# Self attention of a decoder layer: scores formed twice in eight array tiles, exponentials as weights of the value product

## The chip, the cores and the metric

The kernel runs on one core of one Trainium2 chip. The metric is the device time of one execution in microseconds (us). TensorE (PE in the profile) does the matmuls, VectorE (DVE) and ScalarE (ACT) read and write both memories, GpSimd (POOL) works on SBUF alone, and SyncE (SP) issues most DMA transfers. The engines run their own instruction lists in order and meet at semaphores.

## The reference

One decoder layer with pre-normalisation on x of 16 sequences of 64 tokens of 128 features, float32. Cut to what matters:

```
x = x + self_attn(layernorm(x))      # 16 heads of 8, rotary embedding, biases
x = x + cross_attn(layernorm(x), c)  # 8 heads of 64, context of 64 x 96
x = x + moe(layernorm(x))            # 8 experts, top 2, and 2 shared; 128 -> 176 -> 128

# self_attn
q, k, v = x Wq' + bq, x Wk' + bk, x Wv' + bv
q, k = rope(q) * 8**-0.5, rope(k)
out = softmax(q k') v                # per sequence and head: 64 x 64
return out Wo' + bo
```

## The kernel before

The 1024 tokens are 8 tiles of 128 (two sequences each, `NT` = 8) in two halves. Every engine's list is written out by hand; there is no planner. The stages are: normalisation (`statistics`, `inverse_std`, `normalise`, `transpose_xn`), projections (`queries_keys`, `values`, three half-precision passes each, `mm3`), self attention, its output projection (`project_o`), normalisation again (stages 2, 3 of the arrays `LN`), cross attention in eight units, and the experts in 2 x 14 blocks.

Self attention runs in four quads of four sequences. A quad is four units; a unit u = 4 quad + g has four heads (32 of the 128 features, g) of all four sequences. For a unit, `scores` (L1006) is four matmuls with all 128 features contracted: the queries of the other groups are zeroed (`mask_q`, into `qG`), and the keys of each of the four heads stand in a masked copy (`kM`). The result, 128 x 512, has queries on the partitions. VectorE takes the row maxima (L695) and subtracts them into SBUF (L698), ScalarE takes the exponential (L460), TensorE transposes it (`transpose_p`, L1037), ScalarE copies that into `PT` (`copy_t`, L469), and once per quad `attend` multiplies it by masked values (L1058, 32 matmuls on tiles of 32 columns) and by ones for the row sums (L1064). VectorE divides (`divide_ot`, L712, L716), ScalarE adds the value bias (`bias_ot`). Units follow each other about four deep: three banks for scores, two for transposes, one for the product, and banks 6 and 7 (`MISC`) shared in a fixed order by all other products.

Cross attention uses the same functions with units 16 to 23 (`copy_xq`, `scores`, `shift`, `exponentials`, `sums`, `divide` on POOL, `transpose_p`, `copy_t`, `cross_attend`, `cross_project`). `context_keys` (L950) and `context_values` (L990) are float32 products of the context, spread between units.

The expert weights arrive in 13 chunks through two stage buffers. SP starts the transfer of chunk c when `chunk_lo` is at c - 1, that is when POOL has done `split_chunk` (L332) of chunk c - 2. ScalarE first casts the landed chunk (`chunk_float16`, L425), after which POOL may split it. ScalarE's casts are spread over its list by `CHUNK_AT`, one at most per step of the loop over units. The first expert product waits for all 13.

The hand-over to cross attention is `attend(3)`, `divide_ot(3)`, `bias_ot(3)`, `project_o(1)`, `add_x2(1)`, `statistics(3)`, `inverse_std(3)` on POOL, `normalise(3)`, `transpose_xn(2, 1)`, `cross_queries(1)`.

## Time and profile before

| | |
|---|---|
| median of three runs | 193.68 us (191.53 to 193.82) |
| span of the profiled execution | 190.1 us |
| PE, DVE, ACT, POOL busy | 87%, 71%, 61%, 43% |
| mean granted TensorE clock | 0.986 of full speed |

The span goes from the first to the last instruction of one profiled execution, for which no time of its own is given beside the span; the median stands 3.6 us above it. All start times below are counted from the start of the span. A group of matmuls is best timed from its start to the start of the next group, since the ends are modelled. A float32 matmul leaves two records, each with its own weight load. When TensorE is busy throughout a stretch, what the other engines do there costs nothing by itself.

### The profile page before, as it was taken

The page shows a single profiled execution, that of the slowest core. Times are in us where ns is not written, and L with a number is a line of the kernel's source. Part 1 is how long each engine was busy: PE and PEld are TensorE (multiplying, and loading weights), DVE is VectorE, ACT ScalarE, POOL GpSimd, SP SyncE. Part 2 cuts the span into 40 slices and gives each one's busy share as a digit, 9 for nine tenths or more (in the row PEclk, how much of TensorE's full clock was granted, in tenths as well). Part 3 has the DMA queues.
Part 4 walks back from the last instruction along what each step waited for, and adds up shares of the span by engine and source line. Part 5 has one row for each costly group of instructions (what it writes and reads, how often), then busy time and mean ns, then how long its engine had stood idle before and what let it go on. Part 6 is the DMA issues. An engine that isn't in the chain of part 4 may idle for free.

```text
span 190.1 us, 4163 instructions
## 1 busy us (share of the span) xinstructions
PE 165.1 (87%) x1599; PEld 103.2 (54%) x1599; DVE 134.7 (71%) x279; ACT 115.7 (61%) x227; POOL 81.8 (43%) x78
## 2 busy tenths in 40 slices
PE   7576985999999689849999799997998799999992
PEld 2134543665657346635757687653664566666661
DVE  3468998969989627986184554888787987556642
ACT  2148178795788385658779974653649344555450
POOL 1459560847445000763052440074443455544540
PEclk9999999999999999996999999999999999999997
DMA  5980000031221200100000000000000001000001
GB/s 143 304 280 0 0 2 3 0 84 56 59 58 57 78 0 3 59 14 2 10 0 3 2 3 0 0 5 0 0 3 2 0 3 38 17 0 3 2 3 55
DMA packets 6900, 6.43 MB, mean 34 GB/s; under 512 B 736, under 2 KB 5312, under 8 KB 6880
## 3 DMA queue, kind: packets, MB, share of 16 engines
q1 hardware_dynamic: 6480, 5.63, 10.0%
q10 hardware_dynamic: 400, 0.53, 0.9%
q8 instruction: 13, 0.21, 0.5%
q14 instruction: 7, 0.06, 0.1%
HBM read 5.63 MB, written 0.52 MB: 32 GB/s over the span
## 4 chain that ended last, share of the span: by engine, by line
PE 53%; DVE 16%; ACT 14%; issue 7%; POOL 5%; DMA 3%; POOLq 1%; DVEq 0%; ACTq 0%
PE bank L930 6%; PE bank L1006 6%; PE bank L932 6%; PE bank L931 6%; DVE xn_sb L638 4%; PE bank L1175 4%; PE bank L1037 4%; PE bank L1100 4%; ACT Vx L487 3%; PE bank L1110 3%; DMA x_sb<-x_dram 3%; PE bank L1179 2%; POOL rstd L310 2%; PE bank L1159 2%; ACT ex L460 2%
## 5 line engine op out<-in xcount | busy, mean ns | idle before, releaser
L339 POOL TENSOR_TENSOR qG<-qG 128x512 f16<-128x512 f32 (+1 forms) x26 | 30.1, 1157 | 38.4 <-ACT qG L527 38.3
L520 ACT ACTIVATE qG<-bank 128x512 f32<-128x512 f32 (+1 forms) x28 | 16.7, 597 | 24.4 <-PE bank L932 24.4
L798 DVE TENSOR_TENSOR qG<-bank,qG 128x512 f32<-128x512 f32 (+1 forms) x28 | 19.3, 690 | 13.0 <-PE bank L932 11.5
L695 DVE TENSOR_REDUCE mx<-bank 128x8 f32<-128x512 f32 x24 | 16.3, 680 | 6.1 <-PE bank L1022 4.5
L527 ACT CAST qG<-qG 128x512 f16<-128x512 f32 (+1 forms) x28 | 17.1, 612 | 5.5 <-DVE qG L802 3.5
L460 ACT ACTIVATE ex<-sh 128x512 f32<-128x512 f32 x24 | 15.2, 632 | 6.6 <-DVE sh L698 6.5
L1006 PE MATMUL bank<-kM,qG 128*64 128x256 f32 x128 | 16.9, 390 | 1.3 <-DVE qG L679 1.3
L1175 PEld LDWEIGHTS bank<-wd_sb,qG 128*128 128x128 f16 (+1 forms) x224 | 14.7, 98 | 6.2 <-ACT qG L527 0.7
L698 DVE TENSOR_TENSOR sh<-bank,mx 128x512 f32<-128x512 f32 x24 | 16.6, 692 | 1.6 <-ACT ex L460 0.8
L1175 PE MATMUL bank<-wd_sb,qG 128*128 128x128 f16 (+1 forms) x224 | 17.1, 219 | 0.6 <-ACT qG L527 0.6
L802 DVE TENSOR_TENSOR qG<-bank,qG 128x512 f32<-128x512 f32 x22 | 15.2, 692 | 0.7
L1037 PE MATMUL bank<-consts_sb,ex 128*128 128x128 f32 x96 | 14.8, 277 | 0.0
L1037 PEld LDWEIGHTS bank<-consts_sb,ex 128*128 128x128 f32 x96 | 11.1, 141 | 6.3 <-issue 5.3
L332 POOL TENSOR_TENSOR wd_sb<-stage,wd_sb 128x512 f16<-128x512 f32 (+2 forms) x5 | 4.3, 864 | 20.7 <-ACT wd_sb L425 20.7
L487 ACT COPY Vx<-bank 64x256 f32<-64x256 f32 x32 | 11.7, 367 | 2.3 <-PE bank L990 1.9
L346 POOL TENSOR_TENSOR ex<-ex,rs 128x512 f32<-128x512 f32 x8 | 8.4, 1044 | 11.0 <-DVE rs L707 11.0
L469 ACT COPY PT<-bank 128x512 f32<-128x512 f32 x16 | 9.3, 586 | 3.9 <-PE bank L1037 3.8
L950 PE MATMUL bank<-ctxT_sb,xwk_sb 128*128 128x512 f32 x16 | 10.4, 738 | 1.3 <-issue 1.3
L1006 PEld LDWEIGHTS bank<-kM,qG 128*64 128x64 f32 x128 | 8.0, 136 | 6.4 <-issue 2.2
L1100 PE MATMUL bank<-PTx,Vx 128*64 128x128 f32 x128 | 9.6, 296 | 2.0 <-ACT PTx L478 2.0
L414 ACT ACTIVATE kxM<-bank,consts_sb 128x512 f32<-128x512 f32 x16 | 10.0, 684 | 1.7 <-PE bank L950 1.7
L1179 PE MATMUL bank<-wd_sb,qG 128*128 128x128 f16 (+1 forms) x112 | 10.8, 219 | 0.1
(131 smaller groups left out, 380.7 us busy)
## 6 DMA issues: line engine op xcount, KB each, us to landing
stage<-w_gate_dram SPq DMA_DIRECT2D x3, 256.0 KB, 6.6
stage<-w_up_dram SPq DMA_DIRECT2D x3, 256.0 KB, 2.6
stage<-w_down_dram SPq DMA_DIRECT2D x3, 256.0 KB, 2.9
x_sb<-x_dram SPq DMA_DIRECT2D x2, 256.0 KB, 5.7
out_dram<-x_sb SPq DMA_DIRECT2D x2, 256.0 KB, 2.3
ctxT_sb<-ctxT_dram ACTq DMA_DIRECT2D x1, 384.0 KB, 4.7
sel_sb<-selector_dram SPq DMA_DIRECT2D x1, 352.0 KB, 6.4
qG<-attn_w_dram SPq DMA_DIRECT2D x1, 320.0 KB, 5.9
```

What stands on the lines that cost most here:

```text
L339: nc.gpsimd.tensor_tensor(hs[0:r, u % 2, 1, :], hh[0:r, u % 2, :], hs[0:r, u % 2, 0, :], ALU.subtract).then_inc(h_lo, 1)
L460: nc.scalar.activation(ex[:, u % NE, :], sh[:, u % 2, :], ACT.Exp, scale=SCALE1 if u < NU1 else SCALE2).then_inc(e_ready, 1)
L487: ins = nc.scalar.copy(Vx[h2 * S:(h2 + 1) * S, 2 * p + b2, :, :], src)
L520: nc.scalar.activation(sg[0:r, u % 2, :], gbank(u)[0:r, :], ACT.Silu).then_inc(sg_ready, 1)
L527: nc.scalar.copy(hs[0:r, u % 2, 0, :], hh[0:r, u % 2, :]).then_inc(h_hi, 1)
L695: link(nc.vector.reduce_max(mx[:, u % 2, :], v, AX.X))
L698: nc.vector.tensor_tensor(sh[:, u % 2, :].rearrange("p (c t) -> p c t", t=S), v, mx[:, u % 2, :].unsqueeze(2).broadcast_to([P, BLK, S]), A ...
L798: nc.vector.tensor_tensor(dst, ubank(u)[0:r, :], sg[0:r, u % 2, :], ALU.mult).then_inc(hu_ready, 1)
L1006: ins = mm(sbank(u)[b2 * S:(b2 + 1) * S, pp * HG * S:(pp + 1) * HG * S], qG[:, g, b * S:(b + 1) * S], kM[:, b].rearrange("p i t -> p (i t) ...
L1037: ins = nc.tensor.transpose(tbank(u)[:, c * P:(c + 1) * P], ex[:, u % NE, c * P:(c + 1) * P], ident)
L1100: ins = mm(o[c * S:(c + 1) * S, j, :, b2, :], Vx[:, 2 * p + b2, hp, :], PTx[:, u % 2, 2 * hp + b2, :, :], start=True, stop=True)
L1175: mm(pvb[:, n * P:(n + 1) * P], hs[0:r, u % 2, 0, n * P:(n + 1) * P], w[s], start=(first and n == 0 and s == 0), stop=False, skip_group_ch ...
```

## The change

Scores are formed twice. `first_scores` makes them as before in layout, queries on the partitions, but contracts only the 32 features of the group, on array tiles of 32 rows and 64 columns, each group with a bank of its own (0 to 3), so that q needs no mask. `maxima` (VectorE) takes the row maxima of a unit and writes them, 8 per row, into columns of `ms`. After four units `transpose_max` turns these to rows (eight transposes), ScalarE copies them (`copy_mT`), and `shifted_scores` forms the scores again with the keys on the partitions: first minus the maximum (one row contracted, eight matmuls of 512 columns), then k q (sixteen matmuls of 256 columns, q now masked by head) accumulated onto it, in the same banks. ScalarE takes the exponential straight from those banks into `PT`, so the subtraction, the transposes of the exponentials and their copies are gone. `attend` has the exponentials as weights (64 columns) and 18 moving columns: 8 values and a one for each of two sequences, which gives the row sums. `divide_o` divides, `turn_o` transposes back (two transposes), `bias_ot` copies with the bias. `project_o` contracts 64 rows at a time, on the diagonal tiles, with w_o in a new layout.

Around it: the mask of the queries goes from VectorE (first quad) to POOL, all quads; `PTx` now lies in `PT` and is zeroed after the third quad; the raw projection weights are staged in `PT`; a third shared bank (5) joins `MISC`; and every engine's list is written anew. In particular the casts of the weight chunks stand elsewhere in ScalarE's list and the splits elsewhere in POOL's.

```diff
-        VM = sb("VM", [P, 2, NT, G, 2, 32])
+        V1 = sb("V1", [P, NT, H1, 2, D1 + 1])
-        sbank = lambda u: bank[u % 3]
-        tbank = lambda u: bank[3 + u % 2]
+        qbank = lambda g: bank[g]
+        sbank = lambda p: bank[p % 3]
+        tbank = lambda p: bank[3 + p % 2]
+        ob = bank[4]
...
@@ POOL
+            mask_q(0)
+            mask_k(1)
+            mask_q(1)
...
+            mask_k(2)
             mask_q(2)
-            mask_k(2)
+            mask_k(3)
+            mask_q(3)
             for c in range(3):
                 split_chunk(c)
-            mask_q(3)
-            mask_k(3)
-            for c in range(3, 8):
+            pool.wait_ge(pv_full, 3)
+            nc.gpsimd.memset(PT[:, 0:4, :], 0.0).then_inc(zeroed, 1)
+            inverse_std(2)
+            x2_bias(0)
+            for c in range(3, 9):
                 split_chunk(c)
-            inverse_std(2)
-            split_chunk(8)
-            x2_bias(0)
-            for u in range(NU1, NU):
-                divide(u)
-                if u == 16:
+            for p in range(NT):
+                divide(p)
+                if p == 0:
                     inverse_std(3)
-                if u == 17:
+                if p == 1:
                     split_chunk(9)
                     split_chunk(10)
...
@@ ACT
+            def copy_mT(quad):
+                for pp in range(2):
+                    act.wait_ge(mT_full, 2 * quad + pp + 1)
+                    nc.scalar.copy(mT[:, pp].rearrange("p i b s -> p (i b s)"), qbank(pp)[:, :]).then_inc(mT_copied, 1)
...
+            for quad in range(4):
+                copy_mT(quad)
+                if quad == 0:
                     copy_v(0)
...
+                if quad == 3:
+                    copy_cv(2)
+                for g in range(G):
+                    exponentials(4 * quad + g)
...
+                if quad == 1:
+                    bias_ot(0)
+                    copy_v(1)
+                    chunk_float16(0)
+                if quad == 2:
+                    bias_ot(1)
+                    copy_kx(3)
+                    chunk_float16(1)
+                    chunk_float16(2)
+                if quad == 3:
                     bias_ot(2)
+                    copy_cv(3)
+                    chunk_float16(3)
+            copy_kx(4)
+            copy_xnT(2, 0)
+            bias_ot(3)
+            copy_xq(0)
+            copy_kx(5)
+            copy_kx(6)
+            for c in range(4, 8):
+                chunk_float16(c)
+            cross_exponentials(0)
+            chunk_float16(8)
+            cross_exponentials(1)
+            chunk_float16(9)
+            copy_kx(7)
+            copy_t(0)
+            copy_xnT(2, 1)
+            copy_cv(4)
+            cross_exponentials(2)
+            chunk_float16(10)
...
@@ DVE
+            def maxima(u):
+                quad, g = u // 4, u % 4
...
+                dve.wait_ge(first_full, u + 1)
+                nc.vector.reduce_max(ms[:, :, 32 * g], qbank(g)[:, :].rearrange("p (c t) -> p c t", t=S),
+                                     AX.X).then_inc(max_ready, 1)
...
+                if quad == 3:
+                    divide_o(2)
                     add_x2(0)
                     statistics(2, x2_sb)
+                    divide_o(3)
                     normalise(2, x2_sb)
                     rest_xnT(2)
+            shift(0)
+            shift(1)
+            sums(0)
+            add_x2(1)
+            statistics(3, x2_sb)
+            sums(1)
+            normalise(3, x2_sb)
...
@@ PE
+            def first_scores(quad):
...
+                for g in range(G):
+                    if quad:
+                        pe.wait_ge(e_ready, 4 * (quad - 1) + g + 1)
+                    r = slice(32 * g, 32 * (g + 1))
+                    for pp in range(2):
+                        for b2 in range(2):
+                            b = 4 * quad + 2 * pp + b2
+                            t = (2 * pp + b2) * S
+                            ins = mm(qbank(g)[b2 * S:(b2 + 1) * S, pp * HG * S:(pp + 1) * HG * S],
+                                     qr[r, quad % 2, t:t + S], kM[r, b].rearrange("p i t -> p (i t)"),
+                                     start=True, stop=True)
+                    ins.then_inc(first_full, 1)
+
+            def transpose_max(quad):
+                pe.wait_ge(max_ready, 4 * quad + 4)
+                for pp in range(2):
+                    for i in range(HG):
+                        ins = nc.tensor.transpose(qbank(pp)[:, i * P:(i + 1) * P], ms[:, pp * HG + i, :], ident)
+                    ins.then_inc(mT_full, 1)
+
+            def shifted_scores(quad):
+                pe.wait_ge(mT_copied, 2 * quad + 2)
+                pe.wait_ge(q_masked, quad + 1)
+                for b2 in range(2):
+                    for g in range(G):
+                        mm(qbank(g)[b2 * S:(b2 + 1) * S, :], minus_one[32 * g:32 * g + 1, :],
+                           mT[32 * g:32 * g + 1].rearrange("p a i b s -> p (a i) b s")[:, :, b2, :],
+                           start=True, stop=False, skip_group_check=True)
+                for pp in range(2):
+                    for b2 in range(2):
+                        for g in range(G):
+                            r = slice(32 * g, 32 * (g + 1))
+                            t = (2 * pp + b2) * S
+                            ins = mm(qbank(g)[b2 * S:(b2 + 1) * S, pp * HG * S:(pp + 1) * HG * S],
+                                     kr[r, quad % 2, t:t + S], qG[r, :, quad * QT + t:quad * QT + t + S],
+                                     start=False, stop=bool(pp), skip_group_check=True)
+                            if pp and b2:
+                                ins.then_inc(shifted_full, 1)
...
             def attend(quad):
-                pe.wait_ge(t_copied, 4 * quad + 4)
+                pe.wait_ge(e_ready, 4 * quad + 4)
...
+                    pe.wait_ge(ot_ready, quad)
...
+                    for h in range(H1):
+                        ptg = PT[:, (4 * quad + h // HG) % NPT, :].rearrange("p (q i s) -> p q i s", q=2, i=HG)
+                        at = (pp * (H1 // 2) + h // 2) * 2 * (D1 + 1)
+                        ins = mm(ob[h % 2 * S:(h % 2 + 1) * S, at:at + 2 * (D1 + 1)], ptg[:, pp, h % HG, :],
+                                 V1[:, 2 * quad + pp, h].rearrange("p b d -> p (b d)"), start=True, stop=True)
...
+            first_scores(1)
+            attend(0)
+            transpose_max(1)
             context_keys(2)
+            shifted_scores(1)
+            turn_o(0)
+            values(1)
+            queries_keys(3)
+            first_scores(2)
+            attend(1)
+            transpose_max(2)
+            context_values(1)
+            shifted_scores(2)
+            turn_o(1)
             context_keys(3)
+            context_values(2)
+            first_scores(3)
+            attend(2)
+            transpose_max(3)
+            project_o(0)
+            shifted_scores(3)
+            turn_o(2)
+            context_values(3)
+            context_keys(4)
+            attend(3)
+            turn_o(3)
+            transpose_xn(2, 0)
+            cross_queries(0)
+            context_keys(5)
+            cross_scores(0)
+            cross_scores(1)
+            context_keys(6)
+            project_o(1)
+            cross_scores(2)
+            cross_scores(3)
+            context_keys(7)
             transpose_p(0)
+            context_values(4)
+            transpose_xn(2, 1)
+            transpose_p(1)
+            cross_attend(0)
+            cross_queries(1)
...
```

## Rows read from the trace of the kernel before

**Rows 1.** The page, busy us, share of the span and instructions of each engine.
```profile
PE 165.1 (87%) x1599; PEld 103.2 (54%) x1599; DVE 134.7 (71%) x279; ACT 115.7 (61%) x227; POOL 81.8 (43%) x78
```
**Rows 2.** Windows of self attention: stretch, length, busy us (instructions) per engine, clock, DMA.
```profile
core 0: us, PE busy (x) PEld busy (x) DVE busy (x) ACT busy (x) POOL busy (x), PEclk, DMA share, GB/s
32.40:62.00 29.60, 29.60 (x421) 18.26 (x420) 26.19 (x48) 23.23 (x52) 16.75 (x14) 1.00 0.19 53
```
**Rows 3.** Timeline of the start: start us, us, engine, line, operation, idle before.
```profile
16.09 1.71 ACT L452 ACTIVATE kM<-qkr,consts_sb 128x256 f32<-128x256 f32 x4 [0.63 <-DVE qkr L672]
...
19.07 2.81 PE L1006 MATMUL bank<-kM,qG 128*64 128x256 f32 x24 [1.34 <-DVE qG L679]
...
19.72 1.10 DVE L638 TENSOR_SCALAR xn_sb<-x_sb,mv,rstd 128x128 f32<-128x128 f32 x4
```
**Rows 4.** Timeline of TensorE, one unit and one attend.
```profile
43.34 1.10 PE L1058 MATMUL bank<-PT,VM 128*32 128x64 f32 x64
44.26 1.05 PE L1064 MATMUL bank<-PT,consts_sb 128*32 128x256 f32 x16
45.24 0.66 PE L1037 MATMUL bank<-consts_sb,ex 128*128 128x128 f32 x4
45.83 1.08 PE L1006 MATMUL bank<-kM,qG 128*64 128x256 f32 x8
46.84 1.13 PE L990 MATMUL bank<-xwv_sb,ctxT_sb 128*128 128x512 f32 x2
```
**Rows 5.** Timeline of TensorE, groups that follow each other on the full array.
```profile
64.30 1.02 PE L950 MATMUL bank<-ctxT_sb,xwk_sb 128*128 128x512 f32 x2
65.16 0.60 PE L1037 MATMUL bank<-consts_sb,ex 128*128 128x128 f32 x4
65.60 0.38 PE L930 MATMUL bank<-xnT,xwq_sb 128*128 128x512 f16 x1
```
**Rows 6.** Groups by line: count, busy us, mean ns of one, idle before.
```profile
L695 DVE TENSOR_REDUCE mx<-bank 128x8 f32<-128x512 f32 x24 | 16.3, 680 | 6.1 <-PE bank L1022 4.5 <-PE bank L1006 1.4
L698 DVE TENSOR_TENSOR sh<-bank,mx 128x512 f32<-128x512 f32 x24 | 16.6, 692 | 1.6 <-ACT ex L460 0.8
L712 DVE RECIPROCAL rsum<-bank 128x256 f32<-128x256 f32 x4 | 7.0, 1753 | 0.5 <-PE bank L1064 0.4
L469 ACT COPY PT<-bank 128x512 f32<-128x512 f32 x16 | 9.3, 586 | 3.9 <-PE bank L1037 3.8
```
**Rows 7.** A chunk's cast and split (timeline), then transfers: KB, us to landing.
```profile
39.28 0.62 ACT L425 CAST wg_sb<-stage 128x512 f16<-128x512 f32 x1
39.97 1.16 POOL L332 TENSOR_TENSOR wg_sb<-stage,wg_sb 128x512 f16<-128x512 f32 x1 [1.08 <-ACT wg_sb L425]
...
stage<-w_up_dram SPq DMA_DIRECT2D x3, 256.0 KB, 2.6
stage<-w_down_dram SPq DMA_DIRECT2D x3, 256.0 KB, 2.9
```
**Rows 8.** Timeline of the hand-over to cross attention, by engine.
```profile
76.82 1.13 PE L1076 MATMUL bank<-wo_sb,t 128*128 128x128 f32 x8 [0.89 <-ACT t L494]
...
78.64 1.05 POOL L346 TENSOR_TENSOR ex<-ex,rs 128x512 f32<-128x512 f32 x1
80.39 0.23 POOL L308 TENSOR_SCALAR ve<-mv 128x4 f32<-128x4 f32 x1 [0.70 <-DVE mv L627]
80.70 1.04 POOL L310 TENSOR_TENSOR rstd<-ve,minus_half 128x4 f32<-128x4 f32 x1
...
81.78 2.68 DVE L638 TENSOR_SCALAR xn_sb<-x_sb,mv,rstd 128x128 f32<-128x128 f32 x4 [0.52 <-POOL rstd L310]
...
84.61 0.63 PE L959 MATMUL bank<-consts_sb,xn_sb 128*128 128x128 f32 x4 [2.40 <-DVE xn_sb L638]
```
**Rows 9.** Sixteen passes twice (timeline), and the clock in 40 slices (page).
```profile
85.60 1.97 PE L1100 MATMUL bank<-PTx,Vx 128*64 128x128 f32 x16
93.82 1.07 PE L1100 MATMUL bank<-PTx,Vx 128*64 128x128 f32 x16
...
PEclk9999999999999999996999999999999999999997
```

More of the change, by code:

```diff
@@ L182, in decoder_layer @@
         pool_c = sem("pool_c")
[L183 to L184 removed]
+        misc_full = [sem(f"misc_full{i}") for i in range(3)]
+        misc_free = [sem(f"misc_free{i}") for i in range(3)]
         gw_split = sem("gw_split")
@@ new lines, in copy_t @@
+            def copy_t(p):
+                act.wait_ge(t_full, p + 1)
+                if p == 0:
+                    act.wait_ge(zeroed, 5)
+                if p >= 2:
+                    act.wait_ge(pv_full, 4 + p - 2 + 1)
+                src = tbank(p)[:, :].rearrange("p (c s) -> p c s", s=S)
+                for j in range(2):
+                    r = slice(j * S, (j + 1) * S)
+                    ins = nc.scalar.copy(PTx[r, p % 2, :, j, :], src[r])
+                ins.then_inc(t_copied, 1)
@@ new lines, in _ @@
+            copy_xq(1)
+            copy_t(1)
+            copy_otx(0)
+            cross_exponentials(3)
+            copy_cv(5)
+            for p in range(4, NT + 3):
+                if p < NT:
+                    cross_exponentials(p)
+                if p - 2 < NT:
+                    copy_t(p - 2)
+                copy_otx(p - 3)
+                if p in (4, 5):
+                    copy_cv(p + 2)
+                    chunk_float16(p + 7)
+                if p == NT + 1:
+                    copy_xnT(3, 0)
@@ L829, in _ @@
             rotate(0)
-            mask_q0()
             normalise(1, x_sb)
-            for j in range(NU + 4):
-                if j < NU:
-                    shift(j)
-                if 0 <= j - 5 - NU1 < NT:
-                    add_x3(j - 5 - NU1)
-                if NU1 < j < NU and j not in (18, 20):
-                    sums(j - 1)
-                if j == NU - 1:
-                    sums(j)
-                if j == 17:
-                    add_x2(1)
-                    statistics(3, x2_sb)
-                    sums(17)
-                    normalise(3, x2_sb)
-                if j == 0:
+            for quad in range(4):
+                for g in range(G):
+                    maxima(4 * quad + g)
+                if quad == 0:
+                    rest_xnT(1)
                     rotate(1)
-                    rest_xnT(1)
-                if j == 2:
-                    mask_k1()
-                if j == 3:
+                if quad == 1:
                     rotate(2)
-                if j == 8:
-                    rotate(3)
-                if j == 10:
+                    divide_o(0)
                     dve.wait_ge(ld["gw"], 16)
@@ L1074, in project_o @@
                 for n in range(TPH):
-                    t = (hf * TPH + n) * P
-                    ins = mm(ps[:, n * P:(n + 1) * P], OT[:, t:t + P], wo_sb[:, :], start=True, stop=True)
+                    for i2 in range(2):
+                        for b2 in range(2):
+                            r = slice(b2 * S, (b2 + 1) * S)
+                            ins = mm(ps[r, n * P:(n + 1) * P], OT[r, hf * TPH + n, i2, :], wo_sb[r, i2, :],
+                                     start=(i2 == 0), stop=(i2 == 1), skip_group_check=True)
                 ins.then_inc(full, 1)
@@ new lines, in _ @@
+            first_scores(0)
+            transpose_xn(1, 1)
+            queries_keys(1)
+            transpose_max(0)
+            values(0)
+            shifted_scores(0)
+            queries_keys(2)
+            context_values(0)
+            first_scores(1)
+            attend(0)
+            transpose_max(1)
+            context_keys(2)
+            shifted_scores(1)
[4 more added lines that the diff above has]
+            attend(1)
@@ L1256, in _ @@
+            context_values(5)
+            cross_scores(6)
+            cross_project(0)
+            context_values(6)
+            transpose_p(3)
+            cross_attend(2)
+            cross_scores(7)
+            cross_project(1)
+            context_values(7)
+            for p in range(4, NT):
+                transpose_p(p)
+                cross_attend(p - 1)
+                cross_project(p - 2)
             transpose_xn(3, 0)
```

545 lines of the change are left out of this document (212 added, 333 removed).

## The prediction

> **What bounds the kernel now.** I read the busy shares first, then the slices and stretches, then the order of time on each engine where self attention hands over to cross attention. TensorE is busy for 87% of the span [rows 1], and from 32.4 to 62 us, where most of self attention runs, for all 29.60 us of the stretch [rows 2]. So in that stage an edit on VectorE or ScalarE is worth nothing by itself; it must shorten TensorE's list. At two places the stage is set by a chain across engines instead: the start (rotation, mask, first scores) [rows 3], and the hand-over at 76.8 to 84.6 us: `project_o(1)`, the residual, `normalise(3)`, `transpose_xn(2, 1)` [rows 8]. After `transpose_xn(2, 1)` both kernels have the same work in nearly the same order, up to the end. I therefore predict the moment at which that transpose starts (84.61 us now) and carry the difference to the end.
>
> **TensorE, per quad of four units.** Removed: four units of scores at 1.01 us (45.83 to 46.84), four groups of transposes at 0.59 (45.24 to 45.83; where the same tile shape follows they take 0.44 [rows 5]), so about 0.52 on average, and one `attend` at 0.92 + 0.98 (43.34, 44.26, 45.24) [rows 4]. Sum 4.04 + 2.1 + 1.9 = 8.0 us.
> The pieces of the new list come from passes. A float32 matmul is two passes (two records); 512 columns take 0.43 us per pass, since two take 0.86 [rows 5], so 256 columns take 0.213. The four matmuls of a unit are 8 such passes, 1.7 us if they ran in turn; they take 1.01, so the two column halves overlap, with 0.16 for the change of tile shape. The 64 passes of `attend`'s first part (64 columns, 0.053 us each) take 0.92 us, so four column tiles overlap fully [rows 4].
> - `first_scores`: sixteen matmuls of 32x64 tiles. In the written order each row group holds two rounds, and the next group's first round can only join the second one of the group before: five rounds of 2 x 0.213, 2.13 + 0.16 = 2.3 us. If row groups do not overlap it stays at 4 x 1.01 = 4.0; below 1.8 (four rounds) the order excludes.
> - `transpose_max`: 8 transposes at 0.11 [rows 5] = 0.9.
> - `shifted_scores`: eight K = 1 matmuls of 512 columns, all on different tiles, 0.86; then two rounds of eight, 0.86; with the change 1.9. No row shows two row groups at once. The upper end is no overlap: here the row group is the inner loop, so even the column halves no longer pair: 8 x 0.86 + 16 x 0.43 = 13.7. I take 1.9: the nearest rows are the column tiles, which overlap two and four at a time without loss [rows 4], and each row group has a bank of its own.
> - new `attend`: 32 matmuls, 64 passes, 64-column weights, only 18 moving columns. Weight loads are the limit. Lower end: a pass as cheap as now, 0.92 us. Upper end: the present passes load 32 columns each, on four tiles, in 0.92; if only different tiles load at once, twice the columns on half the tiles is four times, 3.7. I take 2.2, near the middle of the two because the present rows are bound by streaming and leave the load between these ends.
> - `turn_o`: 2 x 0.11 + 0.16 = 0.4.
> Sum 7.7 us against 8.0: a saving of 0.3 per quad, 1.2 in all. `project_o` goes from 8 passes on the full array to 32 on 64x64 tiles, two at a time: 16 x 0.107 + 0.16 = 1.85 us instead of 1.13 [rows 8], +1.4 for both. **TensorE's list is as long as before.**
>
> The Trainium skill, TensorE: Matmul & The Clock Gate (Part 3, packing), says that matmuls in different row groups run at once, a four-row packing at 3.07 times; by it `shifted_scores` is 1.9 to 2.5. No row here shows that for rows of the array. The Trainium skill, TensorEngine Tiling (Instruction Overhead), speaks against the 18 moving columns: each matmul costs some 60 cycles whatever its width, which by an estimate is 64 x 25 ns = 1.6 us for the new `attend`; the 64 passes in 0.92 us are already below that floor, so the trace does not bear it out across column tiles [rows 4].
>
> **VectorE and ScalarE.** VectorE loses 16 subtractions (0.69) and four reciprocals of 256 elements (1.75) for ones of 32 elements: 11 + 6 us less [rows 6]. ScalarE loses 16 copies and gains 8 (0.59 each), 4.7 us less [rows 6]. Cover: TensorE's full list hides both, so I count nothing. Masking for q moves from VectorE to POOL: scores start when the key mask ends (16.09 + 1.71 = 17.8) instead of 19.07 [rows 3], -1.2 us; but the projections that filled TensorE there come later.
>
> **The schedule that follows.** A quad's period is 7.7 us plus the projections between (12 half-precision passes of 256 columns at half the float32 price, 1.3, and two float32 matmuls of 512, 1.7) = 10.7. Quad 0 is a bare chain: first scores at 17.8, `normalise(1)` 1.1 to 2.1 and four maxima up to 22, transposes and two copies up to 24.1, shifted scores up to 26, then 2.2 us of projections. So the first scores of quad 1, 2, 3 begin at about 28, 39 and 50; maxima (4 x 0.68), copies and exponentials fit under the other work. Quad 3 has no later quad beside it: exponentials and `bias_ot(2)` hold `attend(3)` until 62, it ends at 64; `normalise(2)` now stands behind `divide_o(3)` on VectorE, so `cross_queries(0)` starts near 68 (65.60 now [rows 5]). `project_o(1)` ends at about 77, against 77.9. The lead from the start is gone by here.
>
> **The step that decides: the weight chunks on ScalarE.** Two stage buffers serve 13 chunks. A chunk can be cast when it has landed; its transfer starts when POOL has split the chunk two before. Now the casts are spread over the kernel. In the new order ScalarE casts chunks 4, 5, 6, 7 in a row after `copy_kx(6)`, then `cross_exponentials(0)`, chunk 8, `cross_exponentials(1)`. `copy_kx(6)` ends at about 76 (its matmul stands ahead of `project_o(1)`). From there, with 0.07 for each handing-over, as 39.90 to 39.97 [rows 7]:
> cast 4 0.69, split 4 1.23, transfer 6 2.67, cast 6 0.67, split 6 1.23, transfer 8 2.97, cast 8 0.67, split 8 1.16 = 11.3 us. Then on POOL `divide(0)` 1.04 and `inverse_std(3)` 1.35, and on VectorE `normalise(3)` 1.1 to 2.7 (2.68 now, beside POOL [rows 8]; the same four instructions took 1.10 with POOL idle [rows 3]). Sum 14.8 to 16.4; 15.5 taken.
> So `transpose_xn(2, 1)` starts at 76 + 15.5 = 91.5 instead of 84.61: **+6.9 us**. Who is queued behind: `cross_exponentials(0)` (shift ready at 74 to 75) waits for casts 6 and 7 until about 82; `sums(0)` and behind it on VectorE `add_x2(1)` and `statistics(3)`; on POOL `divide(0)` and `inverse_std(3)` behind split 8; on TensorE `transpose_p(0)`. SP's queue holds only these transfers.
> TensorE then idles for about 8 us. Now its clock goes to the lower of its two levels, 1.2 GHz, after an idle 2.4 us ending at 84.61 [rows 8]; 16 passes take 1.97 instead of 1.07, and the slice shows a granted 0.6 [rows 9]. It will drop again, earlier; some 10 passes more at half speed: 0 to 2 us, 0.5 taken.
> **Sum:** +7.4 us on the 190.1 span, 197.5. The median of the runs stands 3.6 above the span, which I keep: about 201.0 us.
>
> **Rivals.**
> (a) The chunk wait bites but TensorE's new pieces are at their low ends (`attend` 0.92, first scores 1.8): the period falls by 1.5 before maxima and copies become the bound, `copy_kx(6)` ends near 71.5, transpose at 86.3 to 88: +1.7 to +3.5, 195.4 to 197.2. For it: full overlap of column tiles now. Chance 0.18.
> (b) **Faster**: as (a), and casts 4 to 7 find their chunks ready. They cost 4 x 0.6 = 2.4 us, and the chain from `project_o(1)` (end 73) to the transpose takes the 6.7 us of now: 79.9, -4.7, 189.0. It needs transfer 6 landed when ScalarE comes to it, which the wait of SP on split 4 excludes unless ScalarE is late by some 4 us elsewhere. It decides once the chain from cast 4 is under 8 us. Chance 0.06.
> (c) Weight loads bind: `attend` at 3.7, first scores at 3.0 (between 2.3 and 4.0): +2.2 per quad, three periods and the tail, +8: 209. For it: float32 loads are never seen without a stream over them. Chance 0.15.
> (d) The eight tiles do not run at once: first scores 4.0, shifted 13.7: +13.5 per quad, 54 in all, 255. Against it: column tiles do overlap. Chance 0.05.
>
> **Numbers.** My forecast has 0.56: 201.0 us, itself 197.5 to 205. The range takes in (a) from 195.4 less a little for the schedule, and (c): 194.5 to 209. A change under 2% (3.9 us) cannot be told from none: that is up to 197.6, which holds (a) and a small part of the forecast. Faster 0.06, same 0.20, slower 0.74.
>
> **What would show it.** Right: in the new profile ScalarE idle before the casts of chunks 6 and 8 with a transfer as releaser, 2 to 3 us each; VectorE's `ls` reduction waiting for ScalarE near 80; TensorE idle for 6 us or more ahead of `transpose_xn(2, 1)`, with the granted clock below 1 there. Shifted scores from 1.8 to 2.5 us per quad; the stage from first to last self attention full of TensorE. Wrong: no idle at those casts (b); a shifted group of over 4 us (d); `attend` over 3 us (c). I am also wrong if the work after the transpose has slack that takes up the delay.

## The result, and the profile after

| | before | after |
|---|---|---|
| median of the runs on one chip | 192.9 us (191.53 to 193.82) | 201.95 us (201.16 to 203.9) |
| ratio, 95% interval | | 1.0494 [1.0411, 1.0576] |
| span of the profiled execution | 190.1 us | 202.1 us |
| mean granted TensorE clock | 0.986 | 0.910 |

The change makes the kernel slower by some 5%. The profiled execution of after took 203.9 us and is the longest of its four; the other three have spans of 199.4 to 200.8 us and clocks of 0.932 to 0.949. So start times read from its trace make the delay look 1 to 3 us larger than it typically is.

The page of after, busy shares and the 40 slices:

```profile
PE 166.7 (82%) x1751; PEld 108.1 (53%) x1751; DVE 119.8 (59%) x259; ACT 110.8 (55%) x211; POOL 85.2 (42%) x83
...
PE   7284998989896599406999879998899789999992
...
PEclk9858599999999679965599999999999999999997
```

Against [rows 1], VectorE has lost 15 us of work and ScalarE 5, and the time went the other way. TensorE's busy time rose by only 1.6 us, part of that being passes at the low clock. The two digits to look at are the 4 and the 0 of TensorE, about 81 to 91 us: it stands still for most of that time. Its clock has three low places where [rows 9] has one.

TensorE's timeline in self attention, two first scores and what lies between (half-precision projections left out):

```profile
30.73 1.16 PE L1031 MATMUL bank<-kM,qkr 32*64 32x256 f32 x32
31.82 2.05 PE L1113 MATMUL bank<-V,PT 128*64 128x18 f32 x64
...
34.47 1.09 PE L1041 MATMUL bank<-consts_sb,sh 128*128 128x128 f32 x8 [0.60 <-DVE sh L717]
...
36.35 1.11 PE L1050 MATMUL bank<-ex,consts_sb 1*64 1x512 f32 x16
37.26 1.07 PE L1058 MATMUL bank<-qG,qkr 32*64 32x256 f32 x32
...
38.75 0.44 PE L1121 MATMUL bank<-consts_sb,On 128*128 128x128 f32 x2 [0.42 <-DVE On L746]
...
41.10 1.16 PE L1031 MATMUL bank<-kM,qkr 32*64 32x256 f32 x32
```

`first_scores` takes 31.82 - 30.73 = 1.09 us, `attend` 2.05 and the shifted scores 0.91 + 1.00 = 1.91. From one quad's first scores to the next are 10.4 us here and 10.1 from quad 2 to quad 3 (51.21). TensorE now waits 0.60 us for the maxima in each of the quads 1 to 3 and 0.42 us for `divide_o` in two of them, where it never waited in [rows 2].

The hand-over, TensorE:

```profile
62.62 2.05 PE L1113 MATMUL bank<-V,PT 128*64 128x18 f32 x64 [0.69 <-ACT OT L520]
...
69.36 0.58 PE L957 MATMUL bank<-xnT,xwq_sb 128*128 128x512 f16 x1 [1.52 <-issue]
...
78.04 1.96 PE L1134 MATMUL bank<-wo_sb,OT 64*64 64x128 f32 x32
...
91.63 1.12 PE L1094 MATMUL bank<-consts_sb,ex 128*128 128x128 f32 x4 [8.67 <-POOL ex L358]
...
95.76 1.09 PE L984 MATMUL bank<-consts_sb,xn_sb 128*128 128x128 f32 x4 [1.30 <-DVE xn_sb L671]
```

`project_o(1)` ends near 80, 2 to 3 us later than the forecast (77) and than before (77.9); `transpose_xn(2, 1)` starts at 95.76 against 84.61 in [rows 8]. In between TensorE waits 8.67 us for POOL. The same hand-over on ScalarE, from `copy_kx(6)` on:

```profile
78.15 1.27 ACT L435 ACTIVATE kxM<-bank,consts_sb 128x512 f32<-128x512 f32 x2 [1.69 <-PE bank L975]
79.30 1.14 ACT L446 CAST wu_sb<-stage 128x512 f16<-128x512 f32 x2
83.76 0.62 ACT L446 CAST wu_sb<-stage 128x512 f16<-128x512 f32 x1 [3.32 <-DMA stage<-w_up_dram]
84.65 0.38 ACT L446 CAST wu_sb<-stage 128x224 f16<-128x224 f32 x1 [0.28 <-DMA stage<-w_up_dram]
84.94 0.62 ACT L492 ACTIVATE ex<-sh 128x512 f32<-128x512 f32 x1
88.72 0.62 ACT L446 CAST wd_sb<-stage 128x512 f16<-128x512 f32 x1 [3.16 <-DMA stage<-w_down_dram]
```

and on VectorE and POOL:

```profile
85.59 0.69 DVE L735 TENSOR_REDUCE ls<-ex 128x8 f32<-128x512 f32 x1 [6.63 <-ACT ex L492]
...
92.93 2.68 DVE L671 TENSOR_SCALAR xn_sb<-x_sb,mv,rstd 128x128 f32<-128x128 f32 x4 [2.03 <-POOL rstd L320]
...
89.42 1.16 POOL L344 TENSOR_TENSOR wd_sb<-stage,wd_sb 128x512 f16<-128x512 f32 x1 [3.24 <-ACT wd_sb L446]
...
91.86 1.04 POOL L320 TENSOR_TENSOR rstd<-ve,minus_half 128x4 f32<-128x4 f32 x1
```

Read it from the DMA side: ScalarE waits for chunks 6, 7 and 8 (3.32, 0.28, 3.16 us), its exponentials come late, VectorE's `sums(0)` waits for them, and POOL's `divide(0)` and `inverse_std(3)` stand behind the split of chunk 8. The whole chain from the first of the four casts (79.30) to the transpose is 16.46 us.

Behind the transpose no slack takes up the delay. The first expert product starts here in before and in after:

```profile
119.86 0.38 PE L930 MATMUL bank<-xnT,wg_sb 128*128 128x512 f16 x1
...
131.85 0.38 PE L957 MATMUL bank<-xnT,wg_sb 128*128 128x512 f16 x1
```

The transpose is 11.15 us late, the first expert product 11.99 and the end of the span 12.0.

Windows of after, with the granted clock as the last column but two; rows come in order of time:

```profile
core 0: us, PE busy (x) PEld busy (x) DVE busy (x) ACT busy (x) POOL busy (x), PEclk, DMA share, GB/s
...
18.27:26.54 8.27, 7.44 (x68) 5.91 (x69) 8.20 (x14) 1.76 (x3) 3.36 (x2) 0.59 0.01 2
26.54:62.60 36.06, 32.73 (x594) 21.76 (x593) 20.18 (x45) 23.95 (x52) 20.24 (x15) 1.00 0.07 20
...
66.80:73.60 6.80, 5.27 (x15) 2.07 (x16) 0.69 (x1) 2.50 (x6) 0.00 (x0) 0.51 0.03 11
```

The lower level, 1.2 GHz, holds in parts of the first quad (granted 0.59 on the mean of the row), for 6.8 us that take in `cross_queries(0)` (behind 62.6 to 66.8 us, in which TensorE was busy for 2.48 of 4.20 us), and after the long wait.

### The profile page after: what moved, and what is told of

Read it like the earlier page. It is cut to its first block, busy times and chain, and to the rows that moved or that the text cites. A ratio compares the mean times of both kernels' runs of the same rounds, so it can differ in the third digit from the quotient of the medians.

```text
span 202.1 us, 4385 instructions
## 1 busy us (share of the span) xinstructions
PE 166.7 (82%) x1751; PEld 108.1 (53%) x1751; DVE 119.8 (59%) x259; ACT 110.8 (55%) x211; POOL 85.2 (42%) x83
## 4 chain that ended last, share of the span: by engine, by line
PE 51%; DVE 17%; issue 10%; ACT 10%; POOL 6%; DMA 4%; POOLq 1%; DVEq 0%; ACTq 0%
PE bank L957 7%; PE bank L958 7%; PE bank L959 7%; DVE xn_sb L671 5%; PE bank L1236 4%; PE bank L1161 3%; DVE sh L717 3%; PE bank L1171 3%; DVE t L693 2%; DMA x_sb<-x_dram 2%; PE bank L984 2%; PE bank L975 2%; PE bank L1240 2%; PE bank L1220 2%; PE bank L1080 2%
## 5 line engine op out<-in xcount | busy, mean ns | idle before, releaser
L830 DVE TENSOR_TENSOR qG<-bank,qG 128x512 f32<-128x512 f32 (+1 forms) x28 | 19.3, 690 | 12.9 <-PE bank L959 11.5
L717 DVE TENSOR_REDUCE sh<-bank 128x8 f32<-128x512 f32 x16 | 9.9, 684 | 10.6 <-PE bank L1031 10.6
L735 DVE TENSOR_REDUCE ls<-ex 128x8 f32<-128x512 f32 x8 | 5.5, 682 | 14.9 <-ACT ex L492 14.9
L1094 PE MATMUL bank<-consts_sb,ex 128*128 128x128 f32 x32 | 5.8, 311 | 8.7 <-POOL ex L358 8.7
L335 POOL TENSOR_TENSOR kM<-qkr,consts_sb 128x1024 f32<-128x1024 f32 x3 | 5.7, 1894 | 14.9 <-DVE qkr L707 14.9
L435 ACT ACTIVATE kxM<-bank,consts_sb 128x512 f32<-128x512 f32 x16 | 10.1, 692 | 2.3 <-PE bank L975 2.2
L344 POOL TENSOR_TENSOR wu_sb<-stage,wu_sb 128x512 f16<-128x512 f32 (+1 forms) x4 | 4.0, 1020 | 17.3 <-ACT wu_sb L446 17.3
L1161 PE MATMUL bank<-PT,Vx 128*64 128x128 f32 x128 | 9.6, 296 | 2.0 <-ACT PT L504 2.0
L671 DVE TENSOR_SCALAR xn_sb<-x_sb,mv,rstd 128x128 f32<-128x128 f32 x16 | 8.6, 600 | 3.7 <-POOL rstd L320 3.7
L504 ACT COPY PT<-bank 64x512 f32<-64x512 f32 x16 | 9.3, 580 | 2.7 <-PE bank L1094 2.6
L1220 PE MATMUL bank<-wT,sel_sb 128*128 128x512 f16 x22 | 8.4, 381 | 2.9 <-DVE qG L834 2.9
L984 PE MATMUL bank<-consts_sb,xn_sb 128*128 128x128 f32 x24 | 5.5, 374 | 6.2 <-DVE xn_sb L671 6.2
```

The lines of the kernel that those rows point to most:

```text
L671: ins = nc.vector.tensor_scalar(xn_sb[:, hf, n, :], src[:, hf * TPH + n, :], mv[:, hf, n, 0:1], rstd[:, hf, n:n + 1], ALU.subtract, ALU.mult)
L717: nc.vector.reduce_max(ms[:, :, 32 * g], qbank(g)[:, :].rearrange("p (c t) -> p c t", t=S), AX.X).then_inc(max_ready, 1)
L830: nc.vector.tensor_tensor(dst, ubank(u)[0:r, :], sg[0:r, u % 2, :], ALU.mult).then_inc(hu_ready, 1)
L1161: ins = mm(o[c * S:(c + 1) * S, j, :, b2, :], Vx[:, 2 * p + b2, hp, :], PTx[:, p % 2, 2 * hp + b2, :, :], start=True, stop=True)
```

## The experiments

The theory (A): the bunched casts on two stage buffers hold the exponentials, the sums and POOL, and through them `transpose_xn(2, 1)`. Rivals: (B) TensorE's new list is itself longer or slower; (C) the place of `project_o(1)` and `normalise(2)` in the lists costs it, with the chunks late beside it.

**Five stage buffers**, nothing else moved:

```
-        stage = [sb(f"stage{i}", [P, CH]) for i in range(2)]
+        stage = [sb(f"stage{i}", [P, CH]) for i in range(5)]
...
-                if c >= 2:
-                    sp.wait_ge(chunk_lo, c - 1)
+                if c >= 5:
+                    sp.wait_ge(chunk_lo, c - 4)
```

> The changed kernel with five stage buffers for the weight chunks instead of two; no engine's order is touched. Theory A (ScalarE stands on transfers of chunks 6 and 8, which start only after the splits two before): the idle time of 3.3, 0.3 and 3.2 us before those casts goes, the hand-over is then set by POOL's five splits in a row, transpose_xn(2, 1) starts near 90.3 instead of 95.8, and the time falls by 5 to 6 us, to about 196.5. Rival B (the low TensorE clock and the new tiles set the hand-over, the transfers only stand beside it): less than 1.5 us. Rival C (the delay has slack later in cross attention): the transpose is earlier, the end is not.

Measured: 197.35 us (196.09 to 197.89), ratio to before 1.0237 [1.0140, 1.0333]. ScalarE, POOL and TensorE in it:

```profile
77.76 1.93 ACT L446 CAST wu_sb<-stage 128x512 f16<-128x512 f32 x4
79.59 0.63 ACT L492 ACTIVATE ex<-sh 128x512 f32<-128x512 f32 x1
...
78.45 3.96 POOL L344 TENSOR_TENSOR wu_sb<-stage,wu_sb 128x512 f16<-128x512 f32 x4 [15.29 <-ACT wu_sb L446]
...
88.71 0.63 PE L984 MATMUL bank<-consts_sb,xn_sb 128*128 128x128 f32 x4 [2.61 <-DVE xn_sb L671]
```

The four casts run without a wait, and the transpose is 7.0 us earlier than in after. Of these, 1.5 us lie ahead of the casts (they start at 77.76 instead of 79.30), where this edit does nothing; the chain from the first cast to the transpose is 10.95 us instead of 16.46. 4.6 us of the time are back, and by the ratios to before (1.0494 and 1.0237) that is half of the loss. The bunching isn't gone with the buffers: POOL still has five splits in a row ahead of `divide(0)`, from 78.45 to 83.5. So the waits for transfers make up about half of the loss; this kernel does not say what makes up the rest.

**The casts spread again** (two buffers; casts 4 to 7 one by one between the copies of `kx` and `xq`, 8 and 9 further back, split 8 behind `divide(1)`):

```
             copy_kx(4)
+            chunk_float16(4)
             copy_xnT(2, 0)
             bias_ot(3)
+            chunk_float16(5)
             copy_xq(0)
+            chunk_float16(6)
             copy_kx(5)
+            chunk_float16(7)
             copy_kx(6)
-            for c in range(4, 8):
-                chunk_float16(c)
...
```

> The changed kernel with two stage buffers, but ScalarE's casts of chunks 4 to 9 spread over copy_kx(4) to copy_t(0), and POOL's split of chunk 8 moved behind divide(1). Theory A: no cast waits long, POOL is free for divide(0) and inverse_std(3); transpose_xn(2, 1) starts near 87.6 and the time falls by about 8 us, to 194, within 1% of the kernel before. Rival B: less than 1.5 us. If only the order on POOL counts and not the transfers, this gains and five buffers do not.

Measured: 195.91 us (194.18 to 197.13), ratio 1.0193 [1.0082, 1.0303]. VectorE and TensorE, `add_x2(1)` first:

```profile
80.47 0.65 DVE L759 TENSOR_TENSOR x_sb<-bank,xb_sb 128x512 f32<-128x512 f32 x1
...
83.92 3.54 DVE L674 TENSOR_SCALAR xn_sb<-x_sb,mv,rstd 128x128 f32<-128x128 f32 x4 [0.51 <-POOL rstd L320]
...
87.60 0.63 PE L987 MATMUL bank<-consts_sb,xn_sb 128*128 128x128 f32 x4 [3.68 <-DVE xn_sb L674]
```

and `add_x2(1)` in before:

```profile
78.33 0.65 DVE L724 TENSOR_TENSOR x_sb<-bank,xb_sb 128x512 f32<-128x512 f32 x1
```

6.0 us are back from the order of the casts and of one split alone (0.61 of the loss by the ratios). The time is 1.9 us above what was expected. Three us of the delay against before are left at the transpose. Of these, `add_x2(1)` is 2.14 us late: `project_o(1)` ends at 79.60 instead of 77.88, and `sums(0)` stands ahead of it. The other 0.86 us are `normalise(3)`, 3.54 us beside POOL instead of 2.68. The first part fits (C); this kernel does not test (C) by itself.

**The same fault put into the kernel before** (casts 4 to 7 bunched, splits 3 to 8 behind each other, `mask_q(3)`, `mask_k(3)`, `inverse_std(2)` and `x2_bias(0)` ahead of them on POOL):

```
+                    for c in range(4, 8):
+                        chunk_float16(c)
...
-        CHUNK_AT = [3, 4, 7, 8, 10, 11, 12, 13, 16, 17, 18, 20, 21]
+        CHUNK_AT = {7: (0,), 11: (1, 2), 15: (3,), 16: (8,), 17: (9,), 18: (10,), 20: (11,), 21: (12,)}
```

> The kernel before, with its weight chunks cast and split in the places of the changed kernel (chunks 4 to 7 in a row before the first cross exponential, 8 and 9 behind the next two, splits 3 to 8 ahead of divide). Theory A: chain from cast 4 at 71.2 us gives transpose_xn(2, 1) at 86 to 88 instead of 84.6, and bias_ot(2) is late too: 3 to 5 us slower, 196 to 198. Rival: the bunching costs only together with the new attention; then no change (under 1 us).

Measured: 200.29 us (198.99 to 201.22), ratio 1.0394 [1.0285, 1.0502]. ScalarE and TensorE:

```profile
78.75 0.62 ACT L423 CAST wu_sb<-stage 128x512 f16<-128x512 f32 x1 [2.96 <-DMA stage<-w_up_dram]
79.71 0.62 ACT L423 CAST wu_sb<-stage 128x512 f16<-128x512 f32 x1 [0.34 <-DMA stage<-w_up_dram]
82.63 0.38 ACT L423 CAST wu_sb<-stage 128x224 f16<-128x224 f32 x1 [2.31 <-DMA stage<-w_up_dram]
...
86.15 2.05 PE L1076 MATMUL bank<-wo_sb,t 128*128 128x128 f32 x8 [6.45 <-ACT t L492]
...
94.62 0.63 PE L959 MATMUL bank<-consts_sb,xn_sb 128*128 128x128 f32 x4 [1.43 <-DVE xn_sb L638]
```

Waits of the same kind appear in a kernel that has none of the new matmuls, here before the casts of chunks 5, 6 and 7. They cost 3.9%, and the time is over the 196 to 198 expected: `bias_ot(3)` and with it `project_o(1)` also stand behind the casts, which they do not in after. So the bunching costs without the new matmuls too. It doesn't measure what (B) adds in after; the kernel with the mended order below does.

**The head filled**: `queries_keys(1)` ahead of `first_scores(0)`, so that TensorE has work while the maxima are taken.

```
             queries_keys(0)
-            first_scores(0)
-            transpose_xn(1, 1)
             queries_keys(1)
+            first_scores(0)
+            transpose_xn(1, 1)
...
```

> The changed kernel with queries_keys(1) ahead of first_scores(0), in the 2.3 us for which TensorE stood idle before them. If the head is set by the low clock (transposes of the maxima at 1.7 us instead of 0.9, projections at 2.6 instead of 1.3), the shifted scores of quad 0 start 1 to 2 us earlier and the time falls by as much. Rival: the head is set by VectorE's chain (normalise, maxima); then under 0.5 us.

Measured: 200.25 us (199.82 to 201.59), ratio 1.0408 [1.0312, 1.0505], against 1.0494 for after: 1.7 us back. The start of quad 1 moves from 30.73 to:

```profile
28.43 1.16 PE L1031 MATMUL bank<-kM,qkr 32*64 32x256 f32 x32
```

Not all of that need be the edit. The kernels with five buffers and with spread casts have the old head, and quad 1 starts at 28.99 and 30.04 in their traces; the low clock fell differently in each. The intervals of the two ratios overlap.

**Both edits**, the spread casts and the filled head:

> The changed kernel with the spread casts and splits, and queries_keys(1) ahead of first_scores(0). The two edits act at different places (the hand-over and the head), so they add up: 195.9 less 1.7 = 194.2 us, no different from the kernel before within 1%. If both only moved the phase of the clock, the sum is not reached and the time stays at 195.5 or above.

Measured: 197.16 us (195.05 to 198.06), ratio 1.0249 [1.0161, 1.0337]. The gains do not add: this is no better than the spread alone, and the two intervals overlap. Windows of this kernel:

```profile
10.00:20.00 10.00, 7.08 (x62) 4.18 (x62) 7.88 (x24) 5.14 (x10) 7.47 (x8) 1.00 0.32 118
...
86.60:92.40 5.80, 5.80 (x29) 3.85 (x30) 3.99 (x7) 3.61 (x8) 1.44 (x2) 0.50 0.16 45
```

and the same stretches of the kernel with the spread casts alone:

```profile
10.00:20.00 10.00, 6.32 (x50) 3.59 (x50) 7.74 (x23) 5.13 (x10) 7.38 (x9) 0.67 0.33 120
...
86.60:92.40 5.80, 3.87 (x32) 2.44 (x33) 4.98 (x9) 4.05 (x9) 1.43 (x2) 1.00 0.19 57
```

The low clock has left the start and has come in at 86.6 to 92.4 us, where TensorE is busy throughout. The full clock would have done those 5.8 us of work in about half. The lead of the filled head is smaller: 1.65 us at the start of quad 1 (28.39 against 30.04), 1.0 us at the transpose (86.60 against 87.60). In both kernels TensorE has just waited 3.68 us at the transpose, and only in one of them the clock falls. These are single executions, and the mean clock of this kernel goes from 0.934 to 0.960 from one to the next. That one low spell took the place of the other is seen in these two; why, and how often, is not settled.

**One row group**: all scores use rows 0 to 31 of the array, so row groups cannot overlap. It leaves out that each group needs its own features and maxima. It was timed once.

```
-                    r = slice(32 * g, 32 * (g + 1))
+                    r = slice(0, 32)
...
```

> The changed kernel with all scores on row group 0 (features 0 to 31 for all four groups, so the attention weights are not the reference's); as many matmuls of the same sizes, on two array tiles instead of eight. If the row groups overlap fully in the change, first scores go from 1.1 to 3.6 us a quad and shifted scores from 1.9 to 7.0, +7.6 a quad, +25 to +30 us in all. If the row groups never overlapped (and column halves did), nothing changes.

Measured: 266.85 us, span 265.0, clock 0.828. TensorE's timeline, the first scores of the second quad (`attend` follows at 48.52):

```profile
44.92 3.67 PE L1031 MATMUL bank<-kM,qkr 32*64 32x256 f32 x32
```

and its windows over the shifted scores of the first quad:

```profile
28.78:33.69 4.91, 4.91 (x23) 2.32 (x25) 1.03 (x1) 1.24 (x2) 4.55 (x4) 1.00 0.00 0
33.69:41.60 7.91, 7.91 (x30) 4.07 (x27) 0.00 (x0) 1.57 (x3) 1.29 (x1) 0.50 0.00 0
```

First scores take 3.60 us instead of 1.09. The shifted ones take 4.91 us at the full clock and 7.91 at half of it, 8.9 at the full clock (4.91 + 7.91 / 2) instead of 1.91. So the change does have its eight tiles at work together. The group was expected to take 7.0 and the kernel 25 to 30 us more; it took 64.9 more. That the group takes 8.9 is between two column halves that always pair (7.0) and none that do (the prediction's 13.7), which would be so if some pair; no row shows which. By an estimate the row groups give 4 x (2.5 + 7.0) = 38 us. The clock gives some 27: a mean of 0.828 over 265.0 us holds back 45.6 us, 0.910 over 202.1 us 18.2. It fell to 0.50 at 33.69 us, after 4.91 us in which TensorE was busy throughout, on two of its eight tiles at most.

**Twice the moving columns in `attend`**, 36 instead of 18 (the extra ones are another head's values and make the product a different one). It was timed once.

```
-                        ins = mm(ob[h % 2 * S:(h % 2 + 1) * S, at:at + 2 * (D1 + 1)], ptg[:, pp, h % HG, :],
-                                 V1[:, 2 * quad + pp, h].rearrange("p b d -> p (b d)"), start=True, stop=True)
+                        ins = mm(ob[h % 2 * S:(h % 2 + 1) * S, at:at + 4 * (D1 + 1)], ptg[:, pp, h % HG, :],
+                                 V1[:, 2 * quad + pp, min(h, 14):min(h, 14) + 2].rearrange("p h b d -> p (h b d)"), start=True, stop=True)
```

> The changed kernel with 36 moving columns instead of 18 in each matmul of attend (each overwrites half of its neighbour's, so the output is not the reference's). If attend's 32 ns per pass is the load of 64 float32 weight columns, its 2.05 us stay. If moving columns or their fixed cost set it, it rises: two tiles with 36 columns at two cycles each need 15 ns per pass, so a rise would have to come from there, to 3 us or more.

Measured: 201.03 us, span 199.2, and

```profile
30.13 2.06 PE L1113 MATMUL bank<-V,PT 128*64 128x36 f32 x64
```

18 more moving columns cost nothing. What is left are the 64 weight loads of 64 columns or a fixed cost of each pass; the two are not told apart. Either way a pass takes 32 ns, the change of tile shape included, or 64 ns on each of the two column tiles.

**The order mended**: head filled, `normalise(2)` and `transpose_xn(2, 0)` ahead of `divide_o(3)` and `turn_o(3)`, `project_o(1)` right behind `cross_queries(0)`, `add_x2(1)`, `statistics(3)` and `normalise(3)` ahead of the sums, `inverse_std(3)` on POOL ahead of the divisions, and the casts one at a time. `transpose_xn(2, 1)` itself stands earlier in TensorE's list, ahead of `context_keys(7)`, `cross_scores(3)`, `context_values(4)` and `transpose_p(0)`. The matmuls are those of the change.

```
+            transpose_xn(2, 0)
             turn_o(3)
-            transpose_xn(2, 0)
             cross_queries(0)
+            project_o(1)
             context_keys(5)
             cross_scores(0)
             cross_scores(1)
             context_keys(6)
-            project_o(1)
             cross_scores(2)
+            transpose_xn(2, 1)
+            context_keys(7)
             cross_scores(3)
-            context_keys(7)
+            context_values(4)
             transpose_p(0)
-            context_values(4)
-            transpose_xn(2, 1)
...
+                    normalise(2, x2_sb)
                     divide_o(3)
-                    normalise(2, x2_sb)
                     rest_xnT(2)
+            add_x2(1)
+            statistics(3, x2_sb)
             shift(0)
+            normalise(3, x2_sb)
...
             copy_xq(0)
             copy_kx(5)
+            chunk_float16(5)
+            cross_exponentials(0)
             copy_kx(6)
-            for c in range(4, 8):
-                chunk_float16(c)
...
```

> The changed kernel's instructions in a new order: head filled as above, turn_o behind its cover, normalise(2) and transpose_xn(2, 0) ahead of divide_o(3) and turn_o(3), project_o(1) right after cross_queries(0) (shared bank 5), with add_x2(1), statistics(3) and normalise(3) before any sum, and one cast at most between two exponentials. If the hand-over was only queued work on the wrong side of waits, transpose_xn(2, 1) starts at 76 to 80 us instead of 95.8 and the time is 184 to 190, faster than the kernel before. Rival: ScalarE's list (copies of q, keys, exponentials) is then the bound of this part, little is gained over the spread order: 192 or more.

Measured: **188.36 us** (186.3 to 191.33), ratio to before 0.9715 [0.9595, 0.9835]: faster than both kernels, though the interval does not rule out a gain of under 2%. TensorE:

```profile
68.77 1.96 PE L1140 MATMUL bank<-wo_sb,OT 64*64 64x128 f32 x32
...
76.44 0.63 PE L990 MATMUL bank<-consts_sb,xn_sb 128*128 128x128 f32 x4 [0.67 <-DVE xn_sb L677]
```

and its window of the hand-over:

```profile
62.00:76.00 14.00, 12.53 (x159) 8.01 (x156) 7.10 (x22) 9.79 (x20) 4.17 (x5) 1.00 0.15 40
```

The transpose starts 19.3 us earlier than in after and 8.2 earlier than in before, and the clock holds at 1.00 through the whole hand-over. The time falls by 13.6 us against after and by about 5.5 against before. So rival (B) is answered: the new matmuls do not by themselves make the kernel slower. Of the lead of 8.2 us in the two profiled executions 3.2 are left at the first expert product (116.63 against 119.86) and at the end. The 5 us between are products that stood ahead of the transpose in before and now stand behind it (3.4 us) and longer waits, mostly for ScalarE's copies (5.6 us against 2.8), less the 1.7 us that the low clock held back in before (granted 0.81 over 84.61 to 93.82 us).

**The mended order with five stage buffers:**

> The reordered kernel with five stage buffers. Theory: in the reordered kernel (188.36 us) ScalarE never waits for a chunk any more (its waits from 60 to 95 us are all for products or shifts), so three more buffers are worth nothing: 187.9 to 188.9 us, transpose_xn(2, 1) at 76.0 to 76.9. Rival: a late chunk still holds something that the rows do not name, or the later transfers disturb others: 185 to 187, or over 190.

Measured: 188.19 us (186.43 to 190.1), ratio 0.9710 [0.9618, 0.9802]. As the theory had it, the buffers are worth nothing once no cast waits. The transpose, at 77.87 us, misses its expected 76.9; the profiled execution is the longest of its four (190.1 us).

**The mended order with the old head:**

> The reordered kernel with the changed kernel's head (first_scores(0) ahead of queries_keys(1)). Theory: since the head's gain was lost in the spread version (197.16 against 195.91), the hand-over order is what made the reordered kernel fast, and the head is worth its 1.7 us at most: 188.4 to 190.1 us. Rival: with the waits further on gone, the list of TensorE binds from the head to the end, and the whole 2.3 us by which quad 1 starts later comes back, with more behind it through the clock: 190.7 to 192.5.

Measured: 188.81 us (188.71 to 189.52), ratio 0.9780 [0.9716, 0.9845]; the transpose is at 77.28. The head is worth 0.45 us by the medians and 1.3 us by the ratios to before, the fairer measure here, since before itself stood at 193.8 us beside this kernel and at 193.0 beside the other. Both lie within the intervals. Nearly all of what made the kernel fast is the rest of the new order.

## Why the prediction was right, and where its terms were off

- **The step that decides** was right in place and in kind. Waits of 2 to 3 us at the casts of chunks 6 and 8 were forecast, and are 3.32 and 3.16; `sums(0)` waits as named; TensorE's 8 us are 8.67. The chain of 15.5 us measured 16.46, just over its upper end of 16.4, with `normalise(3)` at its dear price of 2.68. Five buffers and the spread casts show that the bunching is the cause of half to two thirds of the loss (4.6 and 6.0 of 9.0 us); the fault in the old kernel shows that it costs there too. The rest of the loss is put down to the order around it (C), since the mended order brings it all back; that kernel moved many things at once.
- **`copy_kx(6)`** was to end at 76 and ends at 79.42. This is the term that was mis-sized. The prediction had the low clock once, behind the long wait, for 0.5 us. It comes three times: in the first quad (first scores of quad 1 at 30.73 instead of 28, of which it is a part), in `cross_queries(0)`, where 5.27 us of matmuls run at 0.51, and behind the wait. The first two stand ahead of the casts. Of the 2.7 us at the start of quad 1 only 0.6 are left at `attend(3)` (62.62 instead of 62), because the quads were shorter than forecast; `cross_queries(0)` starts 1.4 late (69.36 instead of 68) and takes 4.72 us, where its 12 passes of 512 columns at half the float32 price are 2.6. Together that is the delay of 3.4 us.
- **`first_scores`** was set at 2.3 us, with 1.8 as the least the written order allows. It takes 1.09: 32 passes of 0.213 us on eight tiles are four rounds of one pass each, 0.85, and some 0.2. The trace has the 32 starts of quad 1 in four groups of eight, at 30.73 to 30.81, 30.99 to 31.08, 31.21 to 31.30 and 31.43 to 31.51 us. So a matmul whose tile is busy does not hold those behind it for other tiles, which is what the five rounds rested on. The Trainium skill, TensorE: Matmul & The Clock Gate (Part 3, packing), has matmuls on different row groups run at once; this trace agrees for eight tiles, and the kernel with one row group shows the reverse.
- **Shifted scores** (1.9 forecast, 1.91), `attend` (2.2, 2.05) and `project_o` (1.85, 1.89) were right. For `attend` the Trainium skill, TensorEngine Tiling (Instruction Overhead), gave an estimate of 1.6 us. It measured 2.05, and with twice the moving columns 2.06, so the trace agrees with the Trainium skill that so small a width is not what counts; the size that it gives for the floor is shown by neither kernel.
- **The quad's period** of 10.7 came out at 10.4 and 10.1 because two errors met: the first scores 1.2 us cheaper, and up to 1.0 us of new waits for the maxima and `divide_o`, which the prediction had hidden under other work. They are short tails of chains over three engines that an all-full TensorE had covered.
- **VectorE and ScalarE**: 15 and 5 us less (17 and 4.7 forecast), and the time went up all the same, as forecast.
- **From span to time**: the prediction added 3.6 us, the distance of a median from one span. Every execution on record stands only some 1.8 us above its own span; with that, the profiled execution of before took about 191.9 us by this estimate and was one of the quick ones. The spans of after are 9.3 to 12.0 above 190.1, with a median of 10.05, where 7.4 was forecast. The sum that came out is 190.1 + 10.05 + 1.8 = 201.95. So two errors, a delay 2.6 too small and an offset 1.8 too large, make up the hit within 1 us; that part is luck.
- **After the transpose** the same work in the same time was assumed. It took 106.3 us against 105.5, and from the first expert product on 70.2 us in both.
- **The rivals.** (a) asked for low ends of the new pieces; the first scores had theirs, but the wait decided. (b) needs the chunks ready: it isn't what the change does. In the mended order no cast waits from 60 to 95 us, and the time is 188.36 where (b) had 189.0; but (b) got there with `attend` at 0.92 us, which stayed at 2.05, so the nearness is chance. (c) fell with `attend` at 2.05. (d) fell; the kernel made to behave like it took 266.85 us, where (d) had 255, with a cheaper shifted group (8.9 for 13.7) and a lower clock.

Not settled: which of the mended order's moves brings how much of the 13.6 us (only the head was put back and the buffers were changed one at a time), and what made the clock fall in each place.

## What to carry to other kernels

When a change rewrites the order of an engine's list, look for work that is not part of the change but shares buffers with a slow transfer: a run of casts through two buffers costs a round trip of cast, split and transfer for every two of them, whatever else was gained. Price the new matmuls, but judge the change by the chain at the stage's hand-over, and put into that chain first what the next stage's normalisation needs. And give the new algorithm a schedule of its own before it is judged: with the same matmuls it was 5% slower in one order and 3% faster in another. The old algorithm was given no new order here, so the 3% are not all the algorithm's.

## What the runs showed of the hardware

- Matmuls on eight tiles of 32x64 overlap in both written orders seen here. Row group by row group, 32 float32 passes of 256 columns take 1.09 us, and all on one row group 3.60; with the row group as the inner loop they take 1.00.
- A float32 `attend` pass with 64 weight columns costs 32 ns on two column tiles, with 18 or with 36 moving columns (2.05 and 2.06 us for 64); the old one with 32 weight columns on four tiles 14 ns [rows 4].
- The clock fell to 1.2 GHz (granted 0.50 from 33.69 us) behind 4.91 us in which TensorE was busy throughout, on two of its eight tiles at most.
- The four instructions of `normalise` took 1.10 us with POOL idle [rows 3], 2.68 beside it and 3.54 in the kernel with the spread casts.
